# A sampling-attention kernel: three shifts per axis for every query, the fourth only where it can count, and taps paired from the ninth on

## The reference

```python
off = (q @ W_off + b_off)                  # per query, head, point: a small shift in x and y
attn = softmax(q @ W_attn + b_attn)        # over the 4 points
ix = ref_x * W + off_x - 0.5               # ref_x = linspace(0, 1, 32)
iy = ref_y * H + off_y - 0.5
sampled = bilinear(v, ix, iy)              # zero outside the image
out = (sampled * attn).sum(points) @ W_out + b_out + q
```

## Time and profile before

| | |
|---|---|
| median of 3 runs | 95.16 us (94.81 to 95.44) |
| the profiled execution | 95.24 us, of it a span of 93.4 us from first to last instruction |
| mean granted TensorE clock | 0.922 |
| PE busy | 72.9 us, 78% of the span |
| DVE busy | 65.1 us, 70% |
| POOL busy | 51.7 us, 55% |
| ACT busy | 47.5 us, 51% |

### The profile page before, as it was taken

How to read it: one execution, slowest core, us unless ns; L and a number is a source line. 1 busy time by engine, 2 the same in 40 slices (tenths; PEclk the granted TensorE clock), 3 DMA queues, 4 the chain that set the end, 5 groups by cost and what they waited for, 6 DMA issues and landing times.

```text
span 93.4 us, 1693 instructions
## 1 busy us (share of the span) xinstructions
PE 72.9 (78%) x634; PEld 27.1 (29%) x634; DVE 65.1 (70%) x85; ACT 47.5 (51%) x90; POOL 51.7 (55%) x48
## 2 busy tenths in 40 slices
PE   5999998999499279967999997999999998200000
PEld 4767274122134023313223222212232335100000
DVE  2626979999996705694799679699990016679930
ACT  2201899986999999950000089920000159229600
POOL 7920000959999999972899799999200000007200
PEclk9999999999999985899999999999999999965555
DMA  1939807500089774190000047099960000000095
GB/s 36 274 81 270 305 6 148 152 7 0 0 167 185 167 148 84 40 191 0 0 4 0 7 82 146 0 181 184 189 125 2 0 0 7 0 4 0 4 265 181
DMA packets 3785, 8.51 MB, mean 91 GB/s; under 512 B 576, under 2 KB 1088, under 8 KB 3776
## 3 DMA queue, kind: packets, MB, share of 16 engines
q0 software_dynamic: 1008, 3.67, 21.2%
q1 hardware_dynamic: 2320, 4.03, 15.6%
q10 hardware_dynamic: 448, 0.69, 2.6%
HBM read 2.27 MB, written 1.05 MB: 36 GB/s over the span
## 4 chain that ended last, share of the span: by engine, by line
PE 50%; DVE 14%; issue 9%; DMA 9%; ACT 8%; POOL 5%; DVEq 1%; POOLq 0%
PE banks L482 22%; PE banks L469 14%; DMA prod<-prod 9%; POOL ap L792 5%; ACT tab L641 3%; PE banks L516 3%; PE banks L534 3%; PE banks L464 3%; DVE prod L896 3%; DVE prod L1031 2%; DVE prod L1042 2%; ACT hat L646 2%; PE banks L422 2%; DVE bns L1002 1%; ACT sg L712 1%
## 5 line engine op out<-in xcount | busy, mean ns | idle before, releaser
L792 POOL TENSOR_TENSOR ap<-ays,hat 128x512 f32<-128x512 f32 x30 | 40.1, 1494 | 15.9 <-ACT hat L646 11.3
L896 DVE TENSOR_TENSOR prod<-banks,vpad 128x1024 f32<-128x1024 f32 (+1 forms) x24 | 27.9, 1175 | 10.0 <-PE banks L464 5.5
L482 PE MATMUL banks<-prod,wo 64*64 64x512 f32 x200 | 26.1, 620 | 2.6 <-DMA prod<-prod 2.4
L469 PE MATMUL banks<-ap,cst 32*64 32x512 f32 x160 | 14.1, 609 | 1.8 <-DVE ays L869 1.2
L818 POOL TENSOR_SCALAR prod<-prod,prm,st 128x512 f32<-128x512 f32 x3 | 2.3, 759 | 18.7 <-ACT st L760 18.7
L482 PEld LDWEIGHTS banks<-prod,wo 64*64 64x64 f32 x200 | 6.9, 136 | 19.0 <-issue 11.0
L464 PE MATMUL banks<-ap,cst 64*64 64x512 f32 x80 | 11.4, 647 | 1.2 <-DVE prod L896 1.2
L896 DVE TENSOR_TENSOR prod<-banks,vswap 128x1024 f32<-128x1024 f32 x9 | 10.9, 1214 | 0.0
L641 ACT ACTIVATE tab<-u,cst 128x512 f32<-128x512 f32 x16 | 10.7, 713 | 0.0
L646 ACT ACTIVATE hat<-tab 128x512 f32<-128x512 f32 x16 | 9.2, 621 | 0.0
L799 POOL DMA_DIRECT2D prod<-prod x7 | 8.3, 1188 | 0.2 <-issue 0.2
(11 more groups left out here) (82 smaller groups left out, 80.0 us busy)
## 6 DMA issues: line engine op xcount, KB each, us to landing
prod<-prod POOLq DMA_DIRECT2D x7, 512.0 KB, 4.9
vswap<-vpad SPq DMA_DIRECT2D x4, 342.0 KB, 4.2
xs<-x_dram SPq DMA_DIRECT2D x3, 256.0 KB, 3.8
out_dram<-prod SPq DMA_DIRECT2D x2, 256.0 KB, 3.3
wcf<-w_conv_dram SPq DMA_DIRECT2D x1, 288.0 KB, 4.1
wab<-w_abs_dram SPq DMA_DIRECT2D x1, 288.0 KB, 4.3
xs<-x_dram ACTq DMA_DIRECT2D x1, 256.0 KB, 2.8
out_dram<-prod SPq DMA_DIRECT2D x2, 128.0 KB, 2.8
```

What stands on the lines that cost most here:

```text
L469: mm = pe.matmul(spread_into(t)[quadrant(i, g, t in SWAPPED)[1], g, :], sel_of(g)[rows_in, quadrant(i, g)[1]], weights_at(t)[rows_in], sta ...
L482: mm = pe.matmul(ps_out[g][rows_out], wo[rows_in, rows_in], source[rows_in, g, :], start=False, stop=last, skip_group_check=True)
L792: pool.tensor_tensor(ap[:, j % RAP, :], ays[:, t // TAPS % RY, :], hat[:, yh, 0, kx, :], ALU.mult).then_inc(s_ap, 1)
L896: nc.vector.tensor_tensor(by_half_row(prod[:, t % PR, g, :]), by_half_row(spread_into(t)[:, g, :]), v_window(t, g), ALU.mult).then_inc(s_p, 1)
```

## The change

The taps of a row or column are now the shifts 0, -1, +1 (ZERO, MINUS, PLUS) for all queries, and OUTER: -2 for the first 12 rows or columns and +2 for the last 12. Rows come in the order ZERO, OUTER, MINUS, PLUS and columns in the order ZERO, MINUS, PLUS, OUTER. A tap with one OUTER shift covers 384 of a half's 512 queries and one with two covers 288; its weight, spread, product, sum and projection have that size. Per half that makes 9 taps of 512, 6 of 384 and one of 288.

Besides: `vpad` and `vswap` hold rows of 48 instead of two segments of 19 (3456 elements per partition, was 2736); the OUTER hat is taken from the distance of ZERO (12 distances instead of 16); the flag is computed in 6 parts of 384, 256 and 384 instead of 4 of 512; pairs of taps from t = 8 to 31 (12 pairs, was 9 pairs and 14 single taps), while the third PSUM buffer still comes at t = 12; six sums instead of seven and 26 units instead of 25; new tables for the order of sums, units and rows; `turn(1)` behind tap 5, was 7.

```diff
-FIRST_PAIR = 12
-SPREADS = [(t,) for t in range(FIRST_PAIR)] + [(t, t + 1) for t in range(FIRST_PAIR, LAST - 1, 2)] + [(LAST - 1,), (LAST,)]
+FIRST_PAIR = 8
+THIRD_FROM = 12
+SPREADS = [(t,) for t in range(FIRST_PAIR)] + [(t, t + 1) for t in range(FIRST_PAIR, LAST, 2)]
-SUM_FROM = {0: 1, 4: 5, 8: 9, 16: 18, 20: 22, 21: 23, 24: 26}
-SUM_BEHIND = 6
+SUM_FROM = {1: 2, 5: 6, 8: 10, 16: 18, 20: 22, 24: 26}
+SUMS_BEHIND = {6: 1, 9: 5, 15: 8, 23: 16, 26: 20, 29: 24}
...
+        def size_of(t):
+            n_rows, n_columns = shape_of(t)
+            return n_rows * n_columns
+        def in_zones(ap):
+            return ap.rearrange("p (y s x) -> p y s x", s=2, x=ZONE)
...
-        TAPS_AFTER = {6: [2], 7: [3], 8: [0], 9: [6], 10: [7], 11: [4], 13: [10, 11], 15: [12], 17: [8, 14], 19: [13, 15],
-                      23: [17, 19], 25: [16], 27: [25], 29: [20], 31: [21, 27, 29]}
-        TAPS_AT_END = [24, 28, 30, 31]
+        TAPS_AFTER = {7: [4], 9: [0, 3], 11: [9, 1], 13: [7], 15: [5, 12], 17: [15], 19: [14, 8], 21: [11], 23: [13],
+                      27: [19, 23, 17], 29: [25, 27, 21, 16], 31: [29]}
+        TAPS_AT_END = [24, 28, 30, 20, 31]
...
-                if t == 7:
+                if t == 5:
                     turn(1)
...
-            two_hats(3)
-            two_hats(5)
+            distances(3)
+            hats(3)
+            hats(4)
+            hats(5)
+            distances(4)
+            distances(5)
+            hats(6)
+            hats(7)
...
-            pool.memset(vpad[:].rearrange("p g y a x -> p (g y a x)"), 0.0).then_inc(s_zero, 1)
+            pool.memset(vpad[:].rearrange("p g y x -> p (g y x)"), 0.0).then_inc(s_zero, 1)
...
-            weight(2)
-            weight(3)
-            for t in range(TAPS, NT * YH):
+            for t in range(DVE_COLUMNS[0], NT * YH):
                 weight(t)
-                for into in SUM_FROM:
-                    if SUM_FROM[into] == t - SUM_BEHIND or (t == LAST and SUM_FROM[into] > t - SUM_BEHIND):
-                        sum_products(into)
-                if t == 2 * TAPS - 1:
+                if t in SUMS_BEHIND:
+                    sum_products(SUMS_BEHIND[t])
+                if t == 6:
...
-            ROW_AFTER = [1, 2, 4, 8, 9, 10, 11]
+            ROW_AFTER = [0, 3, 6, 7, 9, 9, 9]
```

More of the change, by code:

```diff
@@ L76, in constants @@
     diff = np.block([[eye, -eye], [-eye, eye]]) * 0.5
-    rows = [j + second, -j, [-(TAP0 + k) for k in range(TAPS)], [0.5, -1.5]]
+    rows = [j, -j, [-SHIFT[k] for k in SHIFT], [0.5, 0.0, -0.5], [-1.5, -1.0, -1.5]]
     rows = np.tile(np.concatenate(rows)[None], (P, 1))
@@ L312, in tap_of @@
             yh, row = divmod(n, TAPS)
-            return yh, ORDER[row], ORDER[column]
+            return yh, ROWS_IN_ORDER[row], COLUMNS_IN_ORDER[column]
         def is_gpsimds(t):
@@ L325, in weights_at, with factors_of @@
         def weights_at(t):
-            return ap[:, own_index(t) % RAP, :] if is_gpsimds(t) else a[:, own_index(t) % RA, :]
+            n = size_of(t)
+            return ap[:, own_index(t) % RAP, 0:n] if is_gpsimds(t) else a[:, own_index(t) % RA, 0:n]
+        def factors_of(t):
+            yh, ky, kx = tap_of(t)
+            factor = ays[:, t // TAPS % RY, rows_of(yh, ky)]
+            if kx == OUTER:
+                first = first_row_of(yh, ky) * 2 * ZONE
+                return both_zones(factor), in_zones(hat[:, yh, 0, kx, first:first + size_of(t)]), in_zones(weights_at(t))
+            return factor, hat[:, yh, 0, kx, rows_of(yh, ky)], weights_at(t)
         def wait_for_hat(engine, yh, d, k):
@@ L355, in deformable_attention_then_binary_conv @@
         UNITS = [unit for t in UNITS_AFTER for unit in UNITS_AFTER[t]] + UNITS_AT_END
-        UPPER_UNITS = UNITS.index(unit_of(15)) + 1
+        UPPER_UNITS = sum(unit[1] < NT for unit in UNITS)
         def units_done(unit, g=G - 1):
@@ L644, in hats @@
                 yh, d, k = HATS[n]
[L645 to L652, removed]
+                m = DISTANCES.index((yh, d, k if k != OUTER else ZERO))
+                act.wait_ge(s_abs, m + 1)
+                if k != OUTER:
+                    nc.scalar.activation(hat[:, yh, d, k, :], tab[:, m % 4], ACT.Relu, bias=1.0, scale=-1.0).then_inc(s_hat, 1)
+                elif d == 1:
+                    at = rows_of(yh, k)
+                    nc.scalar.activation(hat[:, yh, d, k, at], tab[:, m % 4, at], ACT.Relu,
+                                         bias=cst[:, c_tap + PLUS:c_tap + PLUS + 1]).then_inc(s_hat, 1)
+                else:
+                    nc.scalar.activation(in_zones(hat[:, yh, d, k, 0:2 * ZONE * RH]), both_zones(tab[:, m % 4]), ACT.Relu,
+                                         bias=cst[:, c_tap + PLUS:c_tap + PLUS + 1]).then_inc(s_hat, 1)
             def place_x(g, yh):
@@ L697, in _ @@
                 place_x(g, 0)
-            for n in range(8, len(HATS), 2):
-                two_hats(n)
-            for n in range(2 * YH):
+            distances(6)
+            distances(7)
+            hats(8)
+            hats(9)
+            distances(8)
+            hats(10)
+            distances(9)
+            hats(11)
+            distances(10)
+            hats(12)
+            distances(11)
+            hats(13)
+            hats(14)
+            hats(15)
+            for n in range(6):
                 over(n)
@@ L791, in weight @@
                     pool.wait_ge(s_w, taps_of(True)[j - RAP] + 1)
-                pool.tensor_tensor(ap[:, j % RAP, :], ays[:, t // TAPS % RY, :], hat[:, yh, 0, kx, :], ALU.mult).then_inc(s_ap, 1)
+                factor, near, into = factors_of(t)
+                pool.tensor_tensor(into, factor, near, ALU.mult).then_inc(s_ap, 1)
             def sum_products(into):
@@ L877, in weight @@
                     dve.wait_ge(s_w, taps_of(False)[i - RA] + 1)
-                nc.vector.tensor_tensor(a[:, i % RA, :], ays[:, t // TAPS % RY, :], hat[:, yh, 0, kx, :], ALU.mult).then_inc(s_a, 1)
+                factor, near, into = factors_of(t)
+                nc.vector.tensor_tensor(into, factor, near, ALU.mult).then_inc(s_a, 1)
             def product(t):
                 yh, ky, kx = tap_of(t)
-                if yh == 0 and ky == TAPS - 1:
+                if yh == 0 and ky == PLUS:
                     dve.wait_ge(s_vlow, 2)
                 if t in SWAPPED:
-                    for half in range(YH):
+                    for half in range(YH if yh or ky == PLUS else 1):
                         dve.wait_ge(s_vswap[half], 16 * PAIR)
@@ L929, in _ @@
                     softmax_recip(2)
-                if t in ROW_AFTER:
-                    n = ROW_AFTER.index(t) + 1
-                    attend(n)
+                for n in range(1, ROWS):
+                    if ROW_AFTER[n - 1] == t:
+                        attend(n)
             dve.wait_ge(s_f1, 1)
```

137 lines of the change are left out of this document (83 added, 54 removed).

## The result

The changed kernel takes **86.40 us** (median of 3 runs, 85.90 to 86.95), the kernel before 95.16: a ratio of 0.908, 95% interval 0.898 to 0.919. The profiled execution took 85.90 with a span of 84.1. Beside the experiments the kernel before ran 28 more times, and the times fall in two groups: eight took 92.66 to 93.12 us and twenty 94.15 to 95.67, where the three here and its one trace lie as well, so that against the eight (median 92.84) the change gains 6.4 us and not 8.8; what parts the two groups stays open.

The account below looks back on a forecast made before the run. Engines wait for each other from 14.5 to 42.5 us, then PE sets the pace. Pair (12, 13) gains 8.1 us, the later stretch stays near 33.2, the tail unchanged: 95.24 - 8.2 = 87.0 us, range 85.5 to 90.2.

Parts of the forecast that it names:

- case (A): the forecast itself: whole kernel at 87.0 us, own range 86.0 to 88.1, chance 0.56.
- Part 1: POOL's first weights: hat for weight 2 comes 0.6 us earlier, row for weight 4 1.14 + 0.13 earlier.
- Part 2: product 0 to pair (12, 13): 26.0 us falls to 17.6, plus 0.3 for stumbles; pair at 34.4, gain 8.1.
- The price of smaller weights: on POOL: a weight of 384 taken as 0.94 us, between bounds 0.94 (all goes with size) and 1.25 (none).
- Rival (C): POOL's smaller weights cost as much as full ones: 90 us, chance 0.10.
- Rival (E): slower than before, POOL's OUTER column weights in runs of 12 costing 1.3 us more each: near 97, chance 0.06.
- Rival (D): OUTER column, written by PE in runs of 12, costs 0.35 more on each of eight units: 89.5 us, chance 0.06.
- Part 3: pair (12, 13) to last unit's end: 33.2 us against 33.3 before, smaller sizes offset by grown waits.
- The knot: product 28 waits for unit 16 to free tap 16's slot: DVE stands about 5 us, spread 31 late, +1.3 us.
- a sign of being wrong: listed trace signs: PE or DVE gaps over 0.5 us between 28 and 34, or spreads waiting for POOL.
- rival (B): the clock falls once more, in part 2 or around product 28, price 1.5 us: 88.5 us, chance 0.14.
- POOL's lead: POOL runs 1.5 us ahead of the nearly full DVE and PE up to the pair (12, 13).

Follow-up runs that it names:

- e1: kernel before, with only the first DMA sum (unit 0) projected behind tap 11 instead of tap 8: 90.76 us.
- e6: changed kernel with the wait for the first sum put back (DMA behind weight 8, projected behind pair (8, 9)): 92.24 us.
- e10: e6 with SP starting the lower copies into vswap only when the first sum has landed: 87.19 us.
- e2: changed kernel without its sizes (ZONE = 16, every tap 512 queries, flag in 4 parts): 91.02 us.
- e4: changed kernel with unit 16 first instead of last of the four units behind the pair (28, 29): 85.19 us.
- e7: e4 with the DMA of sum 20 started behind weight 28 instead of 26: 83.93 us.
- e5: changed kernel with the row of taps 4 to 7 back behind product 1 instead of product 0: 87.44 us.

## Why the prediction was right

Forecast 87.0 in 85.5 to 90.2; measured 86.4. The forecast case (A) happened, step by step:

- **Part 1.** The first weight comes 0.46 us earlier against product 0 (forecast 0.6), weight 4 1.26 us (1.33).
- **Part 2.** From product 0 to the pair (12, 13): 17.84 us; forecast 17.6, and 17.9 with the 0.3 for stumbles; before 26.02. The idle time went, nothing took its place, and e1, e6 and e10 show that the fall of the clock came from the wait, as the step said. That a sum lands late beside the copies was argued there and is shown now.
- **The price of smaller weights.** 0.96 us for 384, at the low bound. The estimate from the Trainium skill (GPSIMD Engine Reference, section 3.1) was 0.96 as well (1.24 for a full weight from start to start, less 0.28 for 128 elements at 2.6 cycles and 1.2 GHz): the trace agrees. Rival (C) falls with it and with e2. Rival (E) falls with weight 15, 0.94 in runs of 12. Rival (D) falls with units 0 and 3, of which 3 is in runs of 12: they take 1.66 from start to start (29.98 less 28.32), and the prices 0.94 and 0.73 made 1.67.
- **Part 3.** 33.47 us from the pair to the last unit's end; forecast 33.2, before 33.29. The knot is where it was put: a gap of 5.05 us, and e4 gives back 1.5 for the 1.3 I had charged. The sum left out a wait of POOL's: spread 27 stands 0.98 us for it, where I had named a spread that waits for POOL as a sign of being wrong. It is worth little, 0.33 us in e7, since DVE comes next there.
- **The clock**, rival (B), stayed at 1.00 through waits of up to 0.98 us. The Trainium skill (TensorE: Matmul & The Clock Gate, "A second HAM failure mode: psum-queue depth-cycling") warns of a clock that falls again and again by short waits while PE cycles through PSUM buffers. No run here shows such falls: the two that the traces have came behind waits of 2.39 and 4.47 us, and none followed 1.03.
- **Wrong in size:** POOL's lead. I took 1.5 us; at `turn(1)` it is 0.52 and at spread 27 there is none. The 0.4 us that I expected of a late row in e5 rested on it, and it cost 0.96.
- **Not foreseen:** product 0 started 1.05 us earlier. PE's steps from 3.7 us on are 1.04 quicker in that execution, and 0.6 of it are four matmuls with `top_ones` that take 1.27 instead of 1.91. It is scatter between executions and no part of the change, and it is most of the 1.1 us by which the profiled execution, 85.9, beats the forecast; the distance is 51.31, and the forecast made it 51.1. Of all 13 traces the one that I counted from starts product 0 last, which lifts the forecast above the median.
- **The gain** of 8.2 us holds against the traced execution. I took the kernel before to spread over 0.6 us, by three runs; it spreads over 3, and against its shorter executions the same 86.4 is a gain of 6.4.

## What to carry to other kernels

Look for a consumer that stands near its producer in an order written by hand: taking up the first sum three taps later gave 4.15 us in the traces, and 2.1 against the shorter executions, without touching any work. A transfer's time depends on what moves beside it (8.13 or 4.68 us for the same sum), so count from the slow landing, not the median. And after such an edit, walk the queues once more for slots that free late: an engine's gap costs nothing until someone else needs its next result.

## What was not expected

- In the input stage the granted clock reads 1.00 in both traces, yet the same four matmuls take 1.91 us in one and 1.27 in the other; the start of product 0 varies by 1.3 us between executions (15.17 to 16.50), and the end of the tail by 1.0.
- A 512 KB sum lands in 8.13 to 8.27 us beside the lower `vswap` copies, in 4.68 when they are held back, and in a median of 5.4 in the changed kernel.
- Pairs of spreads, each half the passes on paper, gained 0.0 us with two PSUM buffers.
